# A two-stage convolution kernel: the last product of its second group of images worked, evicted and stored in two row parts

## What is computed

```
def _gn(v, G=32, eps=1e-05):        # mean and variance over each channel's 64 x 64 pixels
    g = v.reshape(B_, G, C_ // G, H_, W_)
    m = jnp.mean(g, axis=(2, 3, 4), keepdims=True)
    s = jnp.var(g, axis=(2, 3, 4), keepdims=True)
    return ((g - m) / jnp.sqrt(s + eps)).reshape(v.shape)

# stage 0: a 5x5 and a 3x3 convolution, the latter mixed over nine shifts
x = x + _L0_conv_ref(_gn(x), w3, b3, w5, b5, wr, br)

# stage 1: for every pixel the 9 values of its 3x3 window and a one, all their pairwise
# products (10 x 10), weighted and summed over pairs and input channels
def _L1_conv_ref(x, filters):
    spot = _extract_patches(x, 3, 1, 1)
    spot = jnp.concatenate([ones, spot], axis=-1)
    feat = (spot[..., :, None] * spot[..., None, :]).reshape(spot.shape[:-1] + (100,))
    return jnp.einsum('bcyxf,ocf->boyx', feat, filters.reshape(O, C, 100))
x = x + _L1_conv_ref(_gn(x), filters)
```

## Time and profile before

| | us |
|---|---|
| median of 3 runs | 303.23 |
| the runs | 300.46, 303.23, 304.02 |
| span of the profiled execution | 300.4 |
| TensorE busy in it | 273.3 (91%) |
| VectorE busy | 252.8 (84%) |
| ScalarE busy | 87.6 (29%) |
| GpSimd busy | 29.0 (10%) |

### The profile page before, as it was taken

One profiled execution on the slowest core, in us unless ns is written; L12 is line 12 of the kernel. 1 busy time (PEld: TensorE's weight loads), 2 busy tenths in 40 slices (PEclk: granted clock), 3 DMA queues, 4 the chain that ended last, 5 costly groups with the idle time before them and its releaser, 6 DMA issues.

```text
span 300.4 us, 13567 instructions
## 1 busy us (share of the span) xinstructions
PE 273.3 (91%) x6464; PEld 130.6 (43%) x6464; DVE 252.8 (84%) x216; ACT 87.6 (29%) x135; POOL 29.0 (10%) x82
## 2 busy tenths in 40 slices
PE   0589999899999999999999999999999999999930
PEld 0224343344434433363546475344345446467310
DVE  1899899998999979799999999984999999970330
ACT  4532006979169789539000000004000000000000
POOL 7913920000110000000000000000000000000000
PEclk9999999999999999999999999999999999999995
DMA  6973000000000000000000000085000000000049
GB/s 190 382 203 82 4 2 3 2 5 2 2 2 4 4 2 4 2 2 3 4 2 4 2 4 4 2 171 115 2 2 4 2 2 4 2 4 4 2 91 189
DMA packets 19206, 11.45 MB, mean 38 GB/s; under 512 B 17744, under 2 KB 17872, under 8 KB 19024
## 3 DMA queue, kind: packets, MB, share of 16 engines
q1 hardware_dynamic: 14640, 9.06, 11.9%
q10 hardware_dynamic: 4512, 1.53, 2.2%
HBM read 6.40 MB, written 4.19 MB: 35 GB/s over the span
## 4 chain that ended last, share of the span: by engine, by line
PE 71%; DVE 15%; ACT 4%; issue 3%; DMA 2%; SPq 1%; DVEq 0%
PE acc L1007 63%; PE acc L1050 7%; ACT raw L507 3%; DMA raw<-in_x 2%; DVE stats L741 2%; DVE product L637 2%; DVE plane L759 2%; PE acc L1101 2%; DVE scaled L637 1%; DVE raw L801 1%; DVE product L872 1%; DVE product L663 1%; DVE product L669 1%; DVE arena L669 1%; DVE product L673 1%
## 5 line engine op out<-in xcount | busy, mean ns | idle before, releaser
L1007 PE MATMUL acc<-product,weight 32*32 32x512 f32 (+1 forms) x3072 | 126.8, 604 | 0.3 <-DVE product L872 0.3
L1007 PEld LDWEIGHTS acc<-product,weight 32*32 32x32 f32 (+1 forms) x3072 | 65.2, 110 | 59.4 <-issue 41.5
L879 DVE TENSOR_TENSOR product<-plane 128x4096 f32<-128x4096 f32 x19 | 83.3, 4430 | 0.1
L1007 PE MATMUL acc<-raw,weight 32*32 32x512 f32 (+1 forms) x960 | 45.4, 604 | 0.0
L1050 PE MATMUL acc<-product,middle 32*64 32x512 f32 (+1 forms) x576 | 30.2, 598 | 0.0
L1007 PEld LDWEIGHTS acc<-raw,weight 32*32 32x32 f32 (+1 forms) x960 | 20.7, 112 | 20.2 <-issue 15.7
L801 DVE TENSOR_TENSOR raw<-acc,arena 128x512 f32<-128x512 f32 x16 | 9.9, 683 | 16.7 <-issue 16.6
L1007 PE MATMUL acc<-product,arena 32*32 32x512 f32 (+1 forms) x448 | 22.2, 604 | 0.0
L879 DVE TENSOR_TENSOR raw<-plane 128x4096 f32<-128x4096 f32 x5 | 22.1, 4428 | 0.0
L741 DVE BATCH_NORM_STATS2 stats<-raw 128x6 f32<-128x512 f32 x32 | 19.7, 681 | 2.7 <-DMA raw<-in_x 2.6
L507 ACT ACTIVATE raw<-arena 32x512 f32<-32x512 f32 x32 | 21.8, 681 | 0.5
(11 more groups left out here) (121 smaller groups left out, 209.9 us busy)
## 6 DMA issues: line engine op xcount, KB each, us to landing
raw<-in_x SPq DMA_DIRECT2D x8, 512.0 KB, 8.3
out<-raw SPq DMA_DIRECT2D x24, 128.0 KB, 3.0
arena<-in_L_conv_filters SPq DMA_DIRECT2D x4, 400.0 KB, 6.9
out<-raw ACTq DMA_DIRECT2D x8, 128.0 KB, 4.7
arena<-in_L_conv_w ACTq DMA_DIRECT2D x4, 100.0 KB, 4.0
w_in<-in_L_conv_w ACTq DMA_DIRECT2D x2, 36.0 KB, 1.8
w_in<-in_L_conv_w SPq DMA_DIRECT2D x2, 36.0 KB, 2.2
b_in<-in_L_conv_b SPq DMA_DIRECT2D x2, 0.5 KB
```

Source lines behind the costliest of these rows:

```text
L879: nc.vector.tensor_tensor(both_halves(g, u), plane_halves(g), plane_halves(g, PRODUCTS[k][0] * PITCH + PRODUCTS[k][1]), ALU.mult)\
L1007: return nc.tensor.matmul(acc[32 * s:32 * (s + strips), j, r, :], weights[32 * r:32 * r + 32, t:t + strips, :] .rearrange("p t c -> p (t c ...
```

## The change

For group two alone, the last unit is worked in `LAST_PARTS` = 2 row parts. Part 0 is the first 8 of the 16 rows of each strip (256 of the 512 columns of `acc`), part 1 the last 8. TensorE now does: part 0 even, part 0 odd, part 1 even, part 1 odd, each with three singles and three pairs passes of 256 columns; with the form alternating as before, that is singles, pairs | pairs, singles | singles, pairs | pairs, singles.

After part 0 of a half, `evict` runs as before over all 512 columns of that half: the first 256 are final, the last 256 lack the last unit's product. Part 1 starts its own sum in the freed columns of `acc` (`start` on its first pass), and waits until the half has been evicted. A new `evict_rest` adds these 256 columns to what already stands in `result`. The stores become twice as many of half the size: part 0's behind the odd `evict`, part 1's behind the odd `evict_rest`.

```diff
-        def store(eng, g, r, strips):
+        def store(eng, g, r, strips, part=0, parts=1):
+            size = 2 * CHUNK // parts
             for s in strips:
-                y = SIDE_ROWS * (s // 2) + 1 - s % 2
-                eng.dma_start(out[GROUP * g + r][:, y:y + SIDE_ROWS - 1:2, :],
-                              result[32 * s:32 * s + 32, 2 * CHUNK * r:2 * CHUNK * (r + 1)]
+                y = SIDE_ROWS * (s // 2) + 1 - s % 2 + SIDE_ROWS // parts * part
+                eng.dma_start(out[GROUP * g + r][:, y:y + SIDE_ROWS // parts - 1:2, :],
+                              result[32 * s:32 * s + 32, 2 * CHUNK * r + size * part:2 * CHUNK * r + size * (part + 1)]
                               .rearrange("p (y x) -> p y x", x=W)).then_inc(stored, 16)
...
-            for r in range(GROUP):
-                sp.wait_ge(evicted, 3 * GROUP + r + 1)
-                store(sp, 1, r, (0, 1))
-            sp.wait_ge(stored, 16 * NG * GROUP * STRIPS)
+            for part in range(LAST_PARTS):
+                for r in range(GROUP):
+                    sp.wait_ge(evicted, (3 + 2 * part) * GROUP + r + 1)
+                    store(sp, 1, r, (0, 1), part, LAST_PARTS)
+            sp.wait_ge(stored, 16 * (1 + LAST_PARTS) * GROUP * STRIPS)
...
+            def evict_rest(odd):
+                dve.wait_ge(evicted, (2 + 1 + odd) * GROUP)
+                dve.wait_ge(half_done, 2 + 2 + odd + 1)
+                for r in range(GROUP):
+                    to = view(result, 2 * CHUNK * r + CHUNK + odd, (W, CHUNK // W), (2, HALF_W))
+                    nc.vector.tensor_tensor(to, acc[:, odd, r, CHUNK // 2:CHUNK].rearrange("p (y x) -> p y x", x=HALF_W),
+                                            to, ALU.add).then_inc(evicted, 1)
...
             evict(1, 0)
             evict(1, 1)
+            evict_rest(0)
+            evict_rest(1)
...
-            def column(j, pixels, ys, weights, start, stop, pairs):
+            def column(j, pixels, ys, weights, start, stop, pairs, part=0, parts=1):
                 lo, hi = ys[0], ys[-1]
+                size, rows = CHUNK // parts, SIDE_ROWS // 2 // parts
                 def tile(r, s, strips, d, t, first_one, last_one):
-                    return nc.tensor.matmul(acc[32 * s:32 * (s + strips), j, r, :],
+                    return nc.tensor.matmul(acc[32 * s:32 * (s + strips), j, r, size * part:size * (part + 1)],
                                             weights[32 * r:32 * r + 32, t:t + strips, :]
-                                            .rearrange("p t c -> p (t c)"), pixels(r, SIDE_ROWS * (s // 2) + d),
+                                            .rearrange("p t c -> p (t c)"),
+                                            pixels(r, SIDE_ROWS * (s // 2) + d)[:, rows * part:rows * (part + 1), :],
                                             start=first_one, stop=last_one, tile_position=(32 * r, 32 * s))
...
                 wait_made(g, LAST_UNIT)
-                taps1(g, 0, LAST_UNIT, in_pairs)
-                taps1(g, 0, LAST_UNIT, not in_pairs, True).then_inc(half_done, 1)
-                taps1(g, 1, LAST_UNIT, not in_pairs)
-                taps1(g, 1, LAST_UNIT, in_pairs, True).then_inc(half_done, 1)
+                if g == 0:
...
+                else:
+                    for part in range(LAST_PARTS):
+                        for j in (0, 1):
+                            if part:
+                                pe.wait_ge(evicted, (2 * part + j + 1) * GROUP)
+                            taps1(g, j, LAST_UNIT, in_pairs, False, part, LAST_PARTS, part > 0)
+                            taps1(g, j, LAST_UNIT, not in_pairs, True, part, LAST_PARTS).then_inc(half_done, 1)
+                            in_pairs = not in_pairs
```

More of the change, by code:

```diff
@@ L604, in _ @@
             keep_cross(1)
-            for r in range(GROUP):
-                act.wait_ge(evicted, 3 * GROUP + r + 1)
-                store(act, 1, r, (2, 3))
+            for part in range(LAST_PARTS):
+                for r in range(GROUP):
+                    act.wait_ge(evicted, (3 + 2 * part) * GROUP + r + 1)
+                    store(act, 1, r, (2, 3), part, LAST_PARTS)
         @block.vector
@@ L1181, in side_unit, with taps1 @@
                               start, False, pairs)
-            def taps1(g, j, u, pairs, stop=False):
+            def taps1(g, j, u, pairs, stop=False, part=0, parts=1, start=False):
                 k = 1 if u == NEXT else u - 5
@@ L1190, in taps1 @@
                     last = column(j, stream_pixels(g, u, half, shift), ys,
-                                  weight1[:, at:at + len(ys), :], False, stop and n == len(where) - 1, pairs)
+                                  weight1[:, at:at + len(ys), :], start and n == 0,
+                                  stop and n == len(where) - 1, pairs, part, parts)
                 return last
@@ L1276, in _ @@
                 wait_made(g, LAST_UNIT)
-                taps1(g, 0, LAST_UNIT, in_pairs)
-                taps1(g, 0, LAST_UNIT, not in_pairs, True).then_inc(half_done, 1)
-                taps1(g, 1, LAST_UNIT, not in_pairs)
-                taps1(g, 1, LAST_UNIT, in_pairs, True).then_inc(half_done, 1)
+                if g == 0:
+                    taps1(g, 0, LAST_UNIT, in_pairs)
+                    taps1(g, 0, LAST_UNIT, not in_pairs, True).then_inc(half_done, 1)
+                    taps1(g, 1, LAST_UNIT, not in_pairs)
+                    taps1(g, 1, LAST_UNIT, in_pairs, True).then_inc(half_done, 1)
+                else:
+                    for part in range(LAST_PARTS):
+                        for j in (0, 1):
[4 more added lines that the diff above has]
+                            in_pairs = not in_pairs
 def kernel(**inputs):
```

2 lines of the change are left out of this document (added).

## The result

The changed kernel takes 301.0 us (median of 16 runs, 299.6 to 302.27) against 303.05 us before (16 runs). The ratio is 0.995, 95% interval 0.9935 to 0.9964: faster by 0.5%, 1.5 us, where 3.4 us were forecast (299.9); the two medians lie 2.05 us apart. The direction was right, the size was not.

A forecast was written before the change was run, and what follows sets the result against it. One long TensorE stage, then a tail of stores that nothing overlaps, was taken as the bound. TensorE +2.0, first addition -0.27 and stores -5.1 gave -3.4 us: 299.9 from the median of 303.23, range 296.4 to 302.8.

The forecast's parts named there:

- What bounds the kernel: Whole kernel: one long TensorE stage, busy 91% of 300.4 us, then 12.6 us after the last matmul, about 10.2 of them stores.
- what the tail gives back: After the last matmul: first addition of 256 columns -0.27 us, stores of 1.05 MB instead of 2.10 -5.1 us.
- Rival C: Last stores: they do not halve, issue time decides at 1.15 us each; +1.7 us, 304.9; chance 0.07.
- Its threshold: Last stores: issue time decides from about 0.95 us an issue, where the gain left (2.6) is no more than TensorE's cost.
- The price of a half pass: Last unit on TensorE: 256-column singles pass 0.62 us, pairs pass 0.47; +1.4 and +0.35 us over the full passes.
- A change of form: Last unit, switches between singles and pairs: two more at about 0.15 us each, +0.3 us (bounds +0.2 and +1.2).
- TensorE together: Last unit on TensorE: passes and switches add +2.0 us (bounds +0.2 and +5.8), ending at about 289.8.
- the prediction's own sign of being wrong: Changed profile: TensorE ending after 292 was one of three signs that would make the prediction wrong.
- rival B: Last unit on TensorE: half passes are dear, from more switch drains or showing loads; -1.4 to +0.4 us; chance 0.17.
- What is hidden: Second pair of quarters: the wait for VectorE's evictions costs nothing, with 0.9 us to spare ahead of the odd half.
- Part 0's stores: Sixteen stores (1.05 MB) under TensorE's work: start at 283.3, need 5.1 us, through by about 289.3, ahead of part 1's.
- The base: Starting time: profiled span taken to lie at the fastest of three runs, so the sum came off the median of 303.23.

The follow-up runs named there:

- e2: The kernel before, with group two's stores in two pieces of 8 rows (64 KB) each, nothing else moved; ratio to the kernel before 0.9999.
- e3: The changed kernel with one warm-up round on TensorE in place of three; ratio to the kernel before 0.9984.
- e10: The changed kernel with parts of 10 and 6 rows and 51 one-column matmul calls behind the last warm-up round; ratio to the kernel before 0.9928.
- e7: The changed kernel with parts of 10 and 6 rows in place of 8 and 8; ratio to the kernel before 0.9858.
- e12: The changed kernel with parts of 12 and 4 rows and 51 one-column matmul calls behind the last warm-up round; ratio to the kernel before 0.9996.
- e4: The changed kernel with two warm-up rounds on TensorE in place of three; ratio to the kernel before 0.998.

## Why the prediction was right or wrong

**What bounds the kernel; what the tail gives back.** Right. Tail behind the last matmul 12.6 to 7.4 us, -5.2 for -5.4 forecast: additions of 256 take 0.42 (forecast 0.41), stores of part 1 go from 293.8 to 299.1 at 198 GB/s, 5.3 us for 5.1, and not the 7.6 us that the prediction works out from 138 GB/s. Rival C's issue time fell with e2. Its threshold was misreckoned: at 0.95 us an issue the gain left (2.6 us) is more than TensorE's 2.0, and the sign turns at about 1.06.

**The price of a half pass.** Right in size. Pause-free singles passes come 0.63 to 0.65 apart (forecast 0.62, bounds 0.505 and 0.78), pairs 0.44 (forecast 0.47): 12 x 0.65 - 6 x 1.01 + 12 x 0.444 - 6 x 0.88 = +1.8 for the +1.75 of the sum. The 60 cycles of the Trainium skill (TensorEngine Tiling (Array Packing), Instruction Overhead) would, as an estimate, have put singles at 0.505 + 2 x 0.025 = 0.56; the measured 0.65 decides against it for this form, and the measured 0.44 is under it for pairs. A change of form cost a step of 0.43 at 281.22 against 0.22 usual, +0.2 and not +0.15; but the first singles pass behind a change takes 0.48 and not 0.65, so part of it comes back.

**TensorE together: the step that failed.** "TensorE together: +2.0 us (bounds +0.2 and +5.8)". Measured +3.9, and the prediction's own sign of being wrong, an end of TensorE after 292, came in this trace (292.44; 291.7 without the later start). The sum priced what a matmul costs on its tile and not what 288 calls in place of 144 cost to bring in: 576 instruction places more, in a stretch forecast to grow only from 13.1 to 15.1 us. Three pauses make up the rest: 0.2 (a gap of 0.39 where 0.19 is the rule), 0.5 (3.38 less 2.90) and 1.26 (3.51 less 2.25 in e3), 2.0 us together. 3.9 - 2.0 = 1.9 is left for passes and changes of form. It is in rival B's words, "loads that show between short matmuls", in sign and near its size; its mechanism was not seen. What would have shown it is the page itself: 50 packets of 16 KB on the instruction queue, for TensorE's 6464 matmuls and 6464 loads, are one for each 259 of them, and in TensorE's long stage one starts every 4 to 7 us.

**What is hidden.** The second pair of quarters did not wait for VectorE: the even half's evictions ended at 282.5, and part 1 began at 283.0; the odd half's ended at 285.9, and part 1's odd half began at about 287.4. Held, for the even half with less to spare than said (0.4 us for 0.8), for the odd half with more (1.4 for 0.9, a pause ahead of it included), and in e10, where part 1 is shorter, 0.2 us of it bind.

**Part 0's stores** moved from 285.0 to 292.2, nearly all of them by 291.5, not 284.2 to 289.3. The odd half's evictions came 0.9 us later than forecast (0.8 of it is the later start of the unit in this execution), and the second issue on either queue took 1.5 us. They were through ahead of part 1's (293.8). But they were not free: where they fly, the instruction packet starts about 1 us later (the table).

**The base.** I took the profiled span for the fastest of the runs. A run's time lies 1.8 us above its span, so the profiled execution of before was an ordinary one. It moved no part of the sum.

## What to carry to other kernels

When one matmul is cut into several, price three things: its columns, its fixed part, and its instructions. Count the instructions of the stretch, divide by 256, and compare the time for each 256 with what a fetch takes (here 3.4 to 4.3 us, 4.0 to 4.8 with stores in flight); if the work is shorter, that is the bound. And a gain in the tail is worth its overlap only net of what the overlapped transfers take from instruction fetches: put no border into that stretch if you can. Take the same care elsewhere: calls or waits put in to move a border move all borders behind them, and one can land among other short matmuls.

## What the runs showed of the hardware

- TensorE's instructions arrive in packets of 16 KB, and pauses stand exactly every 128 matmul rows with their loads (256 instructions): at rows 6470, 6598 and 6726 in the traces of kernels whose earlier instructions were the same, and against the work they moved by exactly the 51 or 102 rows' worth put in ahead of it, or the 16 or 32 taken out. In 10 and 6 rows or between long matmuls a border can pass without a pause (0.01 us at e7's 6470).
- A packet starts about 1.1 us after the previous border is passed where pauses stand and no store is ahead of it, and 1.75 to 2.4 us after it with 1250 to 1980 store packets in between; TensorE goes on 2.2 to 3.2 us after the packet's start.
- Two waits became one instruction on TensorE's queue, 105 ns from one to the next: 204 waits made 102.
- The time of a store's issue on a full queue goes with its bytes: 1.15 us for 128 KB, 0.55 us for 64 KB at the same 205 GB/s.
- One-column matmul calls in idle time are not free on average: 51 of them cost 1.2 us (interval 0.3 to 2.2), none in eight runs of 12, and 2 to 4 us in four.
- The granted clock fell to half (1.2 GHz) behind two long pauses of this kind: from 96.31 to 99.72 us in e3, behind 1.93 us of idle, and from 24.79 to 28.20 in e12, in the course of 2.34 us of idle. It fell too in e4, from 18.43 to 21.84, behind 1.77 and 0.70 us of waiting for VectorE. Pauses of 0.25 to 0.68 us at the same rows in other traces had none.
